# Seven experts' weights split ahead of their stage by GpSimd, and the routed products moved to VectorE

## The chip, the cores and the metric

The kernel runs on one core of a Trainium2 chip. Its time is the device time of one execution in microseconds (us); the median of three runs is given, and one further execution was taken with the hardware profiler. Five engines work side by side: TensorE (PE, its weight loads are PEld), VectorE (DVE), ScalarE (ACT), GpSimd (POOL) and SyncE (SP). Each runs its own list of instructions in order, and they wait for one another by semaphores. SP only issues transfers; here POOL issues some too.

## The reference, cut to what matters

2048 tokens of 512 values go through two layers, each a per-sequence matrix and then a feed-forward block, with a residual added:

```python
# layer 0: 2048 hidden values, low-rank terms of 8 experts, top 2 of 8
x = einsum('bct,bcd->bdt', x, weights[conditions])
for k in range(2):
    z1 = (u1 * oh_k).reshape(N, 64)
    h = gelu(x @ W1.T + b1 + z1 @ B1_rf * 2)
    u2 = einsum('nf,erf->ner', h, A2)
    y = h @ W2.T + b2 + (u2 * oh_k) @ B2_rf * 2
    res += w_topk[:, k] * y
# layer 1: 8 routed experts of 352 hidden values (top 2), a shared one of 704
g = silu(x @ w_gate[e]) * (x @ w_up[e])
out = sum_e comb[:, e] * (g @ w_down[e]) + (silu(x @ sw_gate) * (x @ sw_up)) @ sw_down
```

## The kernel before

Every matrix product is done in three products of halves: an f32 matrix is rounded to a high half (a cast to fp32r) and what is left becomes the low half (a subtraction), and high x high, high x low and low x high are summed. So each weight has to be split once on the chip: one cast and one subtraction over it.

**Layer 0** takes four super tiles `s` of 512 tokens, and for each of them 16 hidden tiles `f` of 128: 64 steps. A step of PE is the up product into `ps_h` (L1645 to L1647) and the down product into `ps_y` (L1687 to L1689), each for 512 columns and both choices `k`. ACT applies gelu (L897, L903). DVE then works in a fixed chain for each step: it adds and masks (L1202), and makes `g_hi` and `g_lo` by a cast (L1208) and a subtraction (L1210), and the same for the second choice (L1215 is its subtraction). In `s = 0` ACT casts each tile of W1 and POOL subtracts (`low_w1`, L667); both halves are stored to scratch `w1s_d` and are loaded from there for `s = 1` to `3` (704 KB a step, on SP's queue). From then until near the end of the layer POOL only issues the sequence matrices of layer 1 (`cw1`, `side_col`) in a loop.

**The shared stage** of layer 1 (some 560 to 755 us) computes the shared expert, the gate, and a table of slots: each of 39 slot tiles takes 128 tokens of one expert, by expert. `last_tile[e]` and `etab` tell which tile is of which expert. With these inputs experts 0 to 5 have 5, 4, 6, 4, 4 and 5 slot tiles, so the last tiles are 4, 8, 14, 18, 22 and 27, and experts 6 and 7 share the last eleven.

**The routed stage** (755 to 1032 us) takes one slot tile after the other. For tile `t` on PE: gate product of `t+1` into `ps_h`, transposes of the hidden tile (`turn_g`), up product of `t+1` into `ps_y`, transposes of the gathered rows of `t+2` (`turn_x`), down product. Around it:
- POOL issues `gather(t)` (L744, an indirect DMA of 128 rows of `xc_d` into one of four `xg`) and `scatter_add(t)` (L755, an indirect DMA that adds `yt` into `out`; each waits until the one before it has landed). It also does three operations a tile: `x_low` (L761), the product `rs * ru` (L769) and `g_low` (L773). A scatter is issued one tile later than its `yt` is made.
- ACT casts `xg_hi` (L1002) and copies `xg_f` beside it out of PSUM for POOL, does the silu, copies `ru` (L1016), casts `rgt_hi` (L1020) and copies `rgt_f`, and weighs the result into `yt` (L1030).
- DVE only splits experts 1 to 7: SP loads the raw weights of one (2112 KB, L610 to L614) into `e_raw`, and once the last tile of expert `e-2` is through, DVE splits them in four turns into one of the two buffers of `eg_hi`, `eg_lo`, `ed_hi`, `ed_lo` (L1477 to L1491).

The program ends when the last scatter has landed.

## Time and profile before

| | us |
|---|---|
| median of three runs (lowest, highest) | 1048.93 (1048.3, 1049.98) |
| profiled execution, its time | 1050.06 |
| profiled execution, its span | 1048.2 |

| stage | us of the span | what fills it |
|---|---|---|
| `s = 0` of layer 0, with the splits of W1 | about 40 to 155 | PE, all engines near it |
| layer 0, `s = 1` to `3` | 155 to 545 | PE, 7.39 a step |
| shared stage | 560 to 755.5 | PE |
| routed stage | 755.5 to 1031.7 | PE, 6.9 a tile |
| last scatters | 1031.7 to 1048.2 | indirect DMAs |

The profile's page gives each engine's busy time as a share of the span, then the chain of work that ended last, by engine. Busy shares are averages over stages; what a stage is worth is read in its own rows: windows give busy time by stage, and a timeline gives single instructions with the idle time before each in brackets and what ended it.

### The profile page before, as it was taken

The page shows a single profiled execution, that of the slowest core. Times are in us where ns is not written, and L with a number is a line of the kernel's source. Part 1 is how long each engine was busy: PE and PEld are TensorE (multiplying, and loading weights), DVE is VectorE, ACT ScalarE, POOL GpSimd, SP SyncE. Part 2 cuts the span into 40 slices and gives each one's busy share as a digit, 9 for nine tenths or more (in the row PEclk, how much of TensorE's full clock was granted, in tenths as well). Part 3 has the DMA queues.
Part 4 walks back from the last instruction along what each step waited for, and adds up shares of the span by engine and source line. Part 5 has one row for each costly group of instructions (what it writes and reads, how often), then busy time and mean ns, then how long its engine had stood idle before and what let it go on. Part 6 is the DMA issues. An engine that isn't in the chain of part 4 may idle for free.

```text
span 1048.2 us, 14852 instructions
## 1 busy us (share of the span) xinstructions
PE 1010.6 (96%) x4893; PEld 837.2 (80%) x4895; DVE 524.3 (50%) x886; ACT 314.4 (30%) x550; POOL 354.5 (34%) x351
## 2 busy tenths in 40 slices
PE   8899999999999999999999999999989999999993
PEld 5678887888888887888867777778778999999992
DVE  3788777455565455555566333665543314443000
ACT  3743332211121112111242010301144545454541
POOL 4123245410000000000042000022168889898873
PEclk9999999999999999999999999999999999999997
DMA  7387543443433434453444101005155665665433
GB/s 239 130 297 272 161 136 122 166 161 114 140 123 121 153 128 161 142 181 123 138 159 151 41 1 41 1 1 198 58 187 108 163 163 142 141 146 119 80 61 40
DMA packets 51322, 136.41 MB, mean 130 GB/s; under 512 B 8708, under 2 KB 10004, under 8 KB 50772
## 3 DMA queue, kind: packets, MB, share of 16 engines
q1 hardware_dynamic: 36660, 108.15, 30.1%
q0 software_dynamic: 12432, 25.71, 12.4%
q10 hardware_dynamic: 2192, 2.08, 0.7%
q8 instruction: 19, 0.31, 0.1%
q14 instruction: 19, 0.16, 0.0%
HBM read 96.85 MB, written 39.07 MB: 130 GB/s over the span
## 4 chain that ended last, share of the span: by engine, by line
PE 85%; DVE 4%; POOL 4%; DMA 2%; issue 1%; ACT 1%; ACTq 1%; PEldq 0%; POOLq 0%; PEld 0%; DVEq 0%
PE ps_y L1687 6%; PE ps_y L1689 6%; PE ps_y L1688 5%; PE ps_h L1645 5%; PE ps_h L1647 5%; PE ps_h L1646 5%; PE ps_u L1700 3%; PE ps_u L1699 3%; PE ps_h L1933 2%; PE ps_y L1933 2%; PE ps_y L1928 2%; PE ps_y L1929 2%; PE ps_y L1856 2%; PE ps_y L1857 2%; PE ps_h L1840 2%; PE ps_h L1841 2%
## 5 line engine op out<-in xcount | busy, mean ns | idle before, releaser
L1202 DVE TENSOR_TENSOR h<-h,wb 128x512 f32<-128x512 f32 x64 | 44.4, 693 | 162.6 <-ACT h L903 162.5
L897 ACT ACTIVATE h<-ps_h,bias 128x512 f32<-128x512 f32 x64 | 44.0, 689 | 235.1 <-PE ps_h L1654 235.1
L685 POOL DMA_DIRECT2D s_raw<-in_sgu x8 | 4.3, 544 | 299.9 <-DVE g_lo L1210 192.1
L1687 PE MATMUL ps_y<-w_hi,g_hi 128*128 (+1 forms) x256 | 102.2, 399 | 3.5 <-DVE g_lo L1210 3.5
L1689 PE MATMUL ps_y<-w_hi,g_lo 128*128 (+1 forms) x256 | 101.2, 395 | 0.0
L1688 PE MATMUL ps_y<-w_lo,g_hi 128*128 (+1 forms) x256 | 101.0, 395 | 0.0
L1645 PE MATMUL ps_h<-xt_hi,w_hl 128*128 128x512 f32 x256 | 100.0, 391 | 0.7 <-ACT lg_t L846 0.7
L1647 PE MATMUL ps_h<-xt_hi,w_hl 128*128 128x512 f32 x256 | 100.3, 392 | 0.0
L1646 PE MATMUL ps_h<-xt_lo,w_hl 128*128 128x512 f32 x256 | 100.2, 391 | 0.0
L1477 DVE CAST eg_hi<-e_raw 128x704 fp32r<-128x704 f32 x32 | 16.7, 581 | 138.0 <-PE ps_y L1958 125.3
L903 ACT ACTIVATE h<-ps_h,bias 128x512 f32<-128x512 f32 x64 | 43.9, 688 | 115.4 <-PE ps_h L1667 115.4
L755 POOL DMA_INDIRECT out_x<-yt,slot_tok x39 | 62.7, 1607 | 23.3 <-DMA out_x<-yt,slot_tok 12.5
L761 POOL TENSOR_TENSOR xg_lo<-xg_f,xg_hi 128x512 fp32r<-128x512 f32 x39 | 56.3, 1443 | 17.0 <-ACT xg_f L1005 14.9
L1687 PEld LDWEIGHTS ps_y<-w_hi,g_hi 128*128 128x128 f32 x256 | 48.0, 187 | 15.3 <-DVE g_lo L1210 3.5
L1215 DVE TENSOR_TENSOR g_lo<-h,g_hi 128x512 fp32r<-128x512 f32 x64 | 56.9, 888 | 2.2
L1645 PEld LDWEIGHTS ps_h<-xt_hi,w_hl 128*128 128x128 f32 x256 | 48.1, 188 | 12.2 <-ACT lg_t L846 1.2
L1689 PEld LDWEIGHTS ps_y<-w_hi,g_lo 128*128 128x128 f32 x256 | 48.1, 188 | 11.6
L1688 PEld LDWEIGHTS ps_y<-w_lo,g_hi 128*128 128x128 f32 x256 | 48.1, 188 | 11.5 <-issue 0.2
L1646 PEld LDWEIGHTS ps_h<-xt_lo,w_hl 128*128 128x128 f32 x256 | 48.1, 188 | 11.1
L1647 PEld LDWEIGHTS ps_h<-xt_hi,w_hl 128*128 128x128 f32 x256 | 48.1, 188 | 10.4
L773 POOL TENSOR_TENSOR rgt_lo<-rgt_f,rgt_hi 128x384 fp32r<-128x384 f32 x39 | 52.8, 1353 | 6.8 <-ACT rgt_f L1023 6.8
L1928 PE MATMUL ps_y<-eg_hi,xg_hi 128*128 x156 | 53.5, 345 | 0.0
(319 smaller groups left out, 2455.5 us busy)
## 6 DMA issues: line engine op xcount, KB each, us to landing
w_hl<-w1s_d SPq DMA_DIRECT2D x49, 704.0 KB, 4.1
w1s_d<-w_hl SPq DMA_DIRECT2D x16, 704.0 KB, 5.9
e_raw<-in_wgu SPq DMA_DIRECT2D x8, 1408.0 KB, 7.1
w_raw<-in_w1b SPq DMA_DIRECT2D x16, 608.0 KB, 4.7
xres<-in_x SPq DMA_DIRECT2D x16, 256.0 KB, 4.5
acc<-x_d SPq DMA_DIRECT2D x4, 1024.0 KB, 7.6
xc_d<-xc SPq DMA_DIRECT2D x4, 1024.0 KB, 4.8
e_raw<-in_wdn SPq DMA_DIRECT2D x8, 512.0 KB, 8.4
```

Of the source, the lines that this page charges most:

```text
L755: pool.indirect_dma_start(out=out, in_=yt[t % 4][:], in_offset=None, out_offset=bass.IndirectOffsetOnAxis(ap=slot_tok[:, t:t + 1], axis=0) ...
L761: nc.gpsimd.tensor_tensor(xg_lo[:].rearrange("p c n -> p (c n)"), xg_f[:], xg_hi[:].rearrange("p c n -> p (c n)").bitcast(F32), ALU.subtract)\
L773: nc.gpsimd.tensor_tensor(rgt_lo[:].rearrange("p c n -> p (c n)"), rgt_f[:], rgt_hi[:].rearrange("p c n -> p (c n)").bitcast(F32), ALU.sub ...
L1202: tt(h1[u][:], h1[u][:], wb[:, v, :], ALU.mult).then_inc(gch, 1)
L1215: tt(g1_lo[u][:], h1[u][:], g1_hi[u][:].bitcast(F32), ALU.subtract).then_inc(g1_done, 1)
L1645: mm(ps_h[:, u, :], w_chunk(u, 0, c), xt_hi[v][:, c, :], start=(c == 0), stop=False)
L1646: mm(ps_h[:, u, :], w_chunk(u, 0, c), xt_lo[v][:, c, :], start=False, stop=False)
L1647: mm(ps_h[:, u, :], w_chunk(u, 1, c), xt_hi[v][:, c, :], start=False, stop=False)
L1687: mm(ps_y[:, j, :], g_hi[u][:, cols], sl(w2_hi), start=first, **kw)
L1688: mm(ps_y[:, j, :], g_hi[u][:, cols], sl(w2_lo), start=False, **kw)
L1689: mm(ps_y[:, j, :], g_lo[u][:, cols], sl(w2_hi), start=False, **kw)
L1928: mm(o, xg_hi[:, c, :], w(eg_hi, c), start=(c == 0), stop=False)
```

## The change

- In `s = 1` to `3` of layer 0 POOL takes the weights of experts 1 to 7 in 42 units of 128 x 768 (a host-side layout `we1`, rows padded): it loads a unit (384 KB, `load_unit`), casts it (`high_unit`), stores the high half to scratch `e_d`, subtracts in place (`low_unit`) and stores the low half. There are two buffers for the high halves, and two for the raw ones, three from the ninth unit on (the two more are `u1t`, a tile of layer 0). Unit `k`'s load waits until the down product of step `16 + (k - 2)` is through, so it keeps to one unit a step; the last two stand behind the loads of the shared weights.
- In the routed stage SP loads both halves of an expert straight into the four buffers (`load_halves`, four DMAs, 4352 KB), for `e >= 2` as soon as the last tile of expert `e-2` is through, on the same semaphore that DVE's split had. Expert 1's halves are loaded before the last store of `acc`. DVE's splits of experts 1 to 7 are gone; expert 0 is split as before.
- `x_low`, the product and `g_low` go from POOL to DVE, and read PSUM: ACT's copies `xg_f`, `ru` and `rgt_f` are gone. `xg_hi` and `xg_lo` have two buffers each.
- POOL in the routed stage has gathers and scatters alone, `scatter_add(t)` right behind the wait for its own `yt`.
- PE does `turn_x(0)` in the shared stage, and `turn_x(t+2)` right behind `turn_g(t)`, ahead of the up product.
- `side_col` becomes column 65 of `cw1`: 32 DMAs in place of 64, issued among `low_w1`.

On POOL, in layer 0 behind the last `low_w1`, the loop of small loads stands before, and the shared weights follow at once:

```order
L452 DMA side_col<-in_side 64x1
L672 REGISTER_ALU
L672 COMPARE_AND_BRANCH
L685 DMA s_raw<-in_sgu 128x704 x6
L704 TENSOR_TENSOR sg_lo<-s_raw,sg_hi 128x1408
```

and now the units stand there (`pre_raw`, `u1t` hold raw units, `pre_hi` the high half, `e_d` is the scratch):

```order
L462 DMA cw<-in_cond 64x65
L715 DMA pre_raw<-in_we 128x768
L722 CAST pre_hi<-pre_raw 128x768
L724 DMA e_d<-pre_hi 128x768
L715 DMA u1t<-in_we 128x768
L728 TENSOR_TENSOR pre_raw<-pre_raw,pre_hi 128x768
L731 DMA e_d<-pre_raw 128x768
```

The pattern repeats 42 times, with the next load between the store of the high half and the subtraction.

On POOL in the routed stage, a slot tile before:

```order
L773 TENSOR_TENSOR rgt_lo<-rgt_f,rgt_hi 128x384
L769 TENSOR_TENSOR rg<-rs,ru 128x352
L761 TENSOR_TENSOR xg_lo<-xg_f,xg_hi 128x512
L744 DMA xg<-xc_d,slot_tok 128x512
L755 DMA out_x<-yt,slot_tok 2176x512
```

and now, from the stage's start:

```order
L816 DMA xg<-xc_d,slot_tok 128x512 x2
L838 MEMSET rg 128x32
L816 DMA xg<-xc_d,slot_tok 128x512 x4
L827 DMA out_x<-yt,slot_tok 2176x512
L816 DMA xg<-xc_d,slot_tok 128x512
L827 DMA out_x<-yt,slot_tok 2176x512
```

The first six gathers have no arithmetic between them, and the scatter of a tile is no longer behind the arithmetic of later tiles.

On PE in a slot tile, the end of the up product before, with the transposes of `xg` (`ident,xg`) behind it and ahead of the down product:

```order
L1929 MATMUL ps_y<-eg_lo,xg_hi 128x352
L1933 MATMUL ps_y<-eg_hi,xg_lo 128x352 x4
L1914 MATMUL ps_u<-ident,xg 128x128 x4
L1953 ISA
L1953 MATMUL ps_y<-ed_hi,rgt_hi 128x512
```

and now, where the gate product of the next tile (`ps_h`) ends:

```order
L2006 MATMUL ps_h<-eg_hi,xg_lo 128x352 x4
L2014 MATMUL ps_u<-ident,rg 128x128 x3
L1948 MATMUL ps_u<-ident,xg 128x128 x4
L2001 ISA
L2001 MATMUL ps_y<-eg_hi,xg_hi 128x352
```

The transposes of `xg` have moved ahead of the up product.

The diff, cut to its core:

```diff
+    UNITS, UW = 6, we1.shape[2] // 6
+    AHEAD = UNITS * (E - 1)
+    IN_TWO = 8
+    raw_of = [k % 2 if k < IN_TWO else (k - IN_TWO) % 3 for k in range(AHEAD)]
+    raw_used = [raw_of[:k].count(raw_of[k]) for k in range(AHEAD)]
+    e_d = scr("e_d", (E - 1, 2, UNITS, P, UW))
...
+        ahead = ExitStack()
+        sb_ahead = tensors(ahead)
+        pre_hi = [sb_ahead(f"pre_hi{u}", [P, UW], F32R)[:] for u in range(2)]
+        pre_raw = [sb_ahead("pre_raw0", [P, UW])[:], u1t[:, 0:UW], u1t[:, UW:2 * UW]]
...
-        xg_lo = sb("xg_lo", [P, DC, P], F32R)
-        xg_f = sb("xg_f", [P, DC * P])
+        xg_hi = [sb(f"xg_hi{u}", [P, DC, P], F32R) for u in range(2)]
+        xg_lo = [sb("xg_lo0", [P, DC, P], F32R)]
...
-        def load_matrix(eng, dst, k, width, which, j, h):
-
-            table = (cond0, cond1)[k]
-            off = h * SEQ if width == P else 0
-            b = eng.value_load(it_row[k][0:1, bass.ds(j * 2 + h, 1)], min_val=0, max_val=table.shape[0] // SEQ - 1)
-            eng.dma_start(dst[h * SEQ:(h + 1) * SEQ, bass.ds(j, 1), off:off + SEQ]
-                          .rearrange("p a n -> p (a n)"), table[bass.ds(b * SEQ, SEQ), :]).then_inc(which, 16)
-            if k == 1:
-                eng.dma_start(side_col[h * SEQ:(h + 1) * SEQ, bass.ds(j, 1)],
-                              side[bass.ds(b * SEQ, SEQ), :]).then_inc(which, 16)
+        def load_matrix(eng, j, h):
+
+            at = j * 2 + h
+            b = eng.value_load(it_row[1][0:1, at:at + 1], min_val=0, max_val=cond1.shape[0] // SEQ - 1)
+            eng.dma_start(cw1[h * SEQ:(h + 1) * SEQ, j, :], cond1[bass.ds(b * SEQ, SEQ), :]).then_inc(cw1_in[h], 16)
...
             def load_expert(e):
-                if e:
-                    sp.wait_ge(e_done, e)
...
-            for s in range(NS):
+            def load_halves(e):
+                b = e % 2
+                for k, (eg, ed) in enumerate(((eg_hi, ed_hi), (eg_lo, ed_lo))):
+                    sp.dma_start(eg[:, b].bitcast(F32),
+                                 e_d[e - 1, k, 0:DC, :, 0:2 * H1].rearrange("c p n -> p c n")).then_inc(half_in, 16)
+                    sp.dma_start(ed[:, b].rearrange("p c n -> p (c n)").rearrange("p (c n) -> p c n", n=UW).bitcast(F32),
+                                 e_d[e - 1, k, DC:UNITS].rearrange("c p n -> p c n")).then_inc(half_in, 16)
+
+            for s in range(NS - 1):
                 store_acc(s)
+            for u in range(2):
+                sp.wait_ge(pre_hi_st[u], 16 * (AHEAD // 2))
+            for u in range(3):
+                sp.wait_ge(pre_lo_st[u], 16 * raw_of.count(u))
+            sp.wait_ge(gu_done, NS * SH)
+            load_halves(1)
+            store_acc(NS - 1)
             for e in range(1, E):
-                load_expert(e)
+                if e >= 2:
+                    tiles = sp.value_load(last_tile[0:1, e:e + 1], min_val=0, max_val=SLOT_TILES)
+                    sp.wait_ge(ry_done, 1 + tiles)
+                    load_halves(e)
+                sp.wait_ge(half_in, 64 * e)
+                sp.wait_ge(e_done, e)
+                sp.sem_inc(e_done, 1)
...
             for f in range(FT):
                 low_w1(f, f % 2)
-            with pool.Fori(0, J) as j:
                 for h in range(2):
-                    load_matrix(pool, cw1, 1, SEQ, cw1_in[h], j, h)
-
...
+            pool.wait_ge(w1_lo_done, 2 + FT)
+            pool.wait_ge(w2_lo_done, FT)
+            pool.wait_ge(z_ok, 4)
+
+            def load_unit(k):
+                u = raw_of[k]
+                pool.wait_ge(d_done, 2 + FT + max(k - 2, 0))
+                if u == 2 and not raw_used[k]:
+                    pool.wait_ge(z_ok, 6)
+                if raw_used[k]:
+                    pool.wait_ge(pre_lo_st[u], 16 * raw_used[k])
+                at = k % UNITS * UW
+                pool.dma_start(pre_raw[u], we1[k // UNITS, :, at:at + UW]).then_inc(pre_in[u], 16)
+
+            def high_unit(k):
+                u = k % 2
+                pool.wait_ge(pre_in[raw_of[k]], 16 * (raw_used[k] + 1))
+                if k >= 2:
+                    pool.wait_ge(pre_hi_st[u], 16 * (k // 2))
+                nc.gpsimd.tensor_copy(pre_hi[u], pre_raw[raw_of[k]]).then_inc(pre_hi_done, 1)
+                pool.wait_ge(pre_hi_done, k + 1)
+                pool.dma_start(e_d[k // UNITS, 0, k % UNITS], pre_hi[u].bitcast(F32)).then_inc(pre_hi_st[u], 16)
+
+            def low_unit(k):
+                raw = pre_raw[raw_of[k]]
+                nc.gpsimd.tensor_tensor(raw.bitcast(F32R), raw, pre_hi[k % 2].bitcast(F32), ALU.subtract)\
+                    .then_inc(pre_lo_done, 1)
+                pool.wait_ge(pre_lo_done, k + 1)
+                pool.dma_start(e_d[k // UNITS, 1, k % UNITS], raw).then_inc(pre_lo_st[raw_of[k]], 16)
+
+            def units(ks):
+                for k in ks:
+                    high_unit(k)
+                    if k <= IN_TWO:
+                        load_unit(k + 1)
+                    if IN_TWO <= k < AHEAD - 2:
+                        load_unit(k + 2)
+                    low_unit(k)
+
+            shared_at = (NS - 2) * FT + 2
+            load_unit(0)
+            units(range(shared_at))
...
+            units(range(shared_at, AHEAD))
...
                     pool.wait_ge(a_done, STEPS)
+                    for u in range(3):
+                        pool.wait_ge(pre_lo_st[u], 16 * raw_of.count(u))
...
-            def x_low(t):
-                pool.wait_ge(xg_f_done, t + 1)
-                nc.gpsimd.tensor_tensor(xg_lo[:].rearrange("p c n -> p (c n)"), xg_f[:],
-                                        xg_hi[:].rearrange("p c n -> p (c n)").bitcast(F32), ALU.subtract)\
-                    .then_inc(xg_lo_done, 1)
-
-            def products(t):
-                pool.wait_ge(ru_done, t + 1)
-                if t:
-                    pool.wait_ge(rgt_done, t)
-                nc.gpsimd.tensor_tensor(rg[:, 0:H1], rs[:], ru[:], ALU.mult).then_inc(rg_done, 1)
-
-            def g_low(t):
-                pool.wait_ge(rgt_f_done, t + 1)
-                nc.gpsimd.tensor_tensor(rgt_lo[:].rearrange("p c n -> p (c n)"), rgt_f[:],
-                                        rgt_hi[:].rearrange("p c n -> p (c n)").bitcast(F32), ALU.subtract)\
-                    .then_inc(rgt_lo_done, 1)
...
             pool.wait_ge(xc_st, 16 * NS)
...
             gather(0)
             gather(1)
+            pool.wait_ge(gu_done, NS * SH)
             nc.gpsimd.memset(rg[:, H1:HC * P], 0.0).then_inc(rg_zero, 1)
-            x_low(0)
-            products(0)
-            x_low(1)
             pool.wait_ge(sy_done, NS * TPS)
             for t in range(2, 5):
                 gather(t)
             for t in range(SLOT_TILES):
-                g_low(t)
-                if t + 1 < SLOT_TILES:
-                    products(t + 1)
-                if t + 2 < SLOT_TILES:
-                    x_low(t + 2)
                 if t + 5 < SLOT_TILES:
                     gather(t + 5)
-                if t:
-                    scatter_add(t - 1)
-            scatter_add(SLOT_TILES - 1)
+                scatter_add(t)
...
-            def x_high(t, first=False):
+            def x_high(t, u):
                 act.wait_ge(xgt_done, t + 1)
-                nc.scalar.copy(xg_hi[:].rearrange("p c n -> p (c n)"), ps_u[:, 0, :]).then_inc(xg_hi_done, 1)
-                if not first:
-                    act.wait_ge(xg_lo_done, t)
-                nc.scalar.copy(xg_f[:], ps_u[:, 0, :]).then_inc(xg_f_done, 1)
+                nc.scalar.copy(xg_hi[u][:].rearrange("p c n -> p (c n)"), ps_u[:, 0, :]).then_inc(xg_hi_done, 1)
...
-            def up(t, u):
-                act.wait_ge(rup_done, t + 1)
-                nc.scalar.copy(ru[:], ps_y[:, u, 0:H1]).then_inc(ru_done, 1)
-
...
-                    up(t + 1, 1 - u)
+                g_high(t)
                 if nxt2:
-                    x_high(t + 2)
+                    x_high(t + 2, u)
                 weigh(t, n, stored)
-            x_high(0, first=True)
+            x_high(0, 0)
             silu(0, 0, first=True)
...
                 dve.wait_ge(s_hi_done, n + 1)
                 if n:
                     dve.wait_ge(z_done, 2 + STEPS)
+                else:
+                    for u in range(2):
+                        dve.wait_ge(pre_hi_st[u], 16 * (AHEAD // 2))
+                    for u in range(3):
+                        dve.wait_ge(pre_lo_st[u], 16 * raw_of.count(u))
...
-            for e in range(1, E):
-                dve.wait_ge(e_in, 48 * (e + 1))
-                if e >= 2:
-                    tiles = dve.value_load(last_tile[0:1, e:e + 1], min_val=0, max_val=SLOT_TILES)
-                    dve.wait_ge(ry_done, 1 + tiles)
-                for k in range(4):
-                    split_expert(e, e % 2, k)
+            def x_low(t, u):
+                dve.wait_ge(xg_hi_done, t + 1)
+                tt(xg_lo[u][:].rearrange("p c n -> p (c n)"), ps_u[:, 0, :],
+                   xg_hi[u][:].rearrange("p c n -> p (c n)").bitcast(F32), ALU.subtract).then_inc(xg_lo_done, 1)
+
+            def products(t, u, first=False):
+                dve.wait_ge(rs_done, t + 1)
+                dve.wait_ge(rup_done, t + 1)
+                if not first:
+                    dve.wait_ge(rgt_done, t)
+                tt(rg[:, 0:H1], rs[:], ps_y[:, u, 0:H1], ALU.mult).then_inc(rg_done, 1)
+
+            def g_low(t):
+                dve.wait_ge(rgt_hi_done, t + 1)
+                tt(rgt_lo[:].rearrange("p c n -> p (c n)"), ps_u[:, 1, 0:HC * P],
+                   rgt_hi[:].rearrange("p c n -> p (c n)").bitcast(F32), ALU.subtract).then_inc(rgt_lo_done, 1)
+
+            def slot_tile(t, u, nxt=True, nxt2=True):
+                g_low(t)
+                if nxt2:
+                    x_low(t + 2, u)
+                if nxt:
+                    products(t + 1, 1 - u)
+
+            x_low(0, 0)
+            x_low(1, 1)
...
                         slot_sums(0)
+                    if (s, j) == (NS - 1, 0):
+                        turn_x(0, 0, 16, first=True)
...
+                        pe.wait_ge(rg_done, t - 1)
...
                 if nxt:
                     gate_or_up(t + 1, 1 - u, after, 0)
                 turn_g(t)
+                if nxt2:
+                    turn_x(t + 2, x_buf, n)
                 if nxt:
                     gate_or_up(t + 1, 1 - u, after, 1)
-                if nxt2:
-                    turn_x(t + 2, x_buf, n)
                 down_routed(t, u, this)
             pe.wait_ge(rg_zero, 1)
-            turn_x(0, 0, 16, first=True)
             e = experts(0)
             gate_or_up(0, 0, e[0], 0)
+            turn_x(1, 1, 16)
```

## Rows read from the trace of the kernel before

**Rows 1.** The page: busy us (share) by engine; share of the last chain

```profile
PE 1010.6 (96%) x4893; PEld 837.2 (80%) x4895; DVE 524.3 (50%) x886; ACT 314.4 (30%) x550; POOL 354.5 (34%) x351
...
PE 85%; DVE 4%; POOL 4%; DMA 2%; issue 1%; ACT 1%; ACTq 1%; PEldq 0%; POOLq 0%; PEld 0%; DVEq 0%
```

**Rows 2.** Windows: span, busy PE, PEld, DVE, ACT, POOL, PE clock, DMA share, GB/s

```profile
190.00:427.00 237.00, 236.64 (x1030) 191.92 (x1029) 133.71 (x227) 45.93 (x69) 15.07 (x29) 1.00 0.40 136
755.48:773.44 17.96, 13.97 (x73) 11.82 (x72) 4.98 (x6) 5.79 (x12) 10.12 (x10) 0.92 0.67 224
773.00:1022.00 249.00, 246.32 (x1444) 227.25 (x1443) 73.09 (x94) 123.05 (x252) 216.57 (x177) 1.00 0.54 125
```

**Rows 3.** Timeline, layer 0: start, duration us, instruction [idle before, what ended it]

```profile
382.12 0.69 DVE L1202 TENSOR_TENSOR h<-h,wb 128x512 f32<-128x512 f32 x1 [3.72 <-ACT h L903]
...
384.03 0.69 DVE L1210 TENSOR_TENSOR g_lo<-h,g_hi 128x512 fp32r<-128x512 f32 x1
...
386.27 0.39 PE L1687 MATMUL ps_y<-w_hi,g_hi 128*128 x1
...
389.51 0.69 DVE L1202 TENSOR_TENSOR h<-h,wb 128x512 f32<-128x512 f32 x1 [3.72 <-ACT h L903]
```

**Rows 4.** Timeline, layer 0, s = 0: POOL's W1 subtraction beside DVE's subtraction

```profile
140.48 1.75 POOL L667 TENSOR_TENSOR w_hl<-w_raw,w_hl 128x640 fp32r<-128x640 f32 x1
...
140.83 1.95 DVE L1215 TENSOR_TENSOR g_lo<-h,g_hi 128x512 fp32r<-128x512 f32 x1
```

**Rows 5.** Costs by line: duration ns min/median/max, first and last start us, forms

```profile
L1215 DVE TENSOR_TENSOR g_lo<-h,g_hi x64: 691/694/1946, 52.6 to 529.2; 128x512 fp32r<-128x512 f32 x64
```

**Rows 6.** Timeline, routed stage: POOL's subtraction with DVE idle

```profile
822.80 1.28 POOL L761 TENSOR_TENSOR xg_lo<-xg_f,xg_hi 128x512 fp32r<-128x512 f32 x1
```

**Rows 7.** DMA issues: KB each, median us from issue to landing

```profile
w_hl<-w1s_d SPq DMA_DIRECT2D x49, 704.0 KB, 4.1
...
e_raw<-in_wgu SPq DMA_DIRECT2D x8, 1408.0 KB, 7.1
...
s_raw<-in_sgu POOLq DMA_DIRECT2D x8, 352.0 KB, 3.9
```

**Rows 8.** Timeline, PE, entry of the routed stage

```profile
755.48 0.60 PE L1914 MATMUL ps_u<-ident,xg 128*128 128x128 f32 x4
...
762.86 0.42 PE L1928 MATMUL ps_h<-eg_hi,xg_hi 128*128 x1 [0.92 <-ACT xg_hi L1002]
...
769.62 0.65 PE L1914 MATMUL ps_u<-ident,xg 128*128 128x128 f32 x4 [2.01 <-DMA xg<-xc_d,slot_tok]
...
773.44 0.49 PE L1928 MATMUL ps_h<-eg_hi,xg_hi 128*128 x1
```

**Rows 9.** Timeline, PE: first gate matmul of slot tiles 36, 38; last down product

```profile
1008.26 0.33 PE L1928 MATMUL ps_h<-eg_hi,xg_hi 128*128 x1
...
1021.75 0.33 PE L1928 MATMUL ps_h<-eg_hi,xg_hi 128*128 x1
...
1029.56 0.49 PE L1953 MATMUL ps_y<-ed_hi,rgt_hi 128*128 x1 [0.96 <-ACT rgt_hi L1020]
```

**Rows 10.** Timeline, the last scatters (POOL) and the last yt (ACT)

```profile
1028.37 0.69 ACT L1030 ACTIVATE yt<-ps_y,slot_w 128x512 f32<-128x512 f32 x1 [1.71 <-PE ps_y L1958]
1032.02 0.69 ACT L1030 ACTIVATE yt<-ps_y,slot_w 128x512 f32<-128x512 f32 x1 [2.21 <-PE ps_y L1958]
1033.71 1.58 POOL L755 DMA_INDIRECT out_x<-yt,slot_tok  x1 [2.81 <-DMA out_x<-yt,slot_tok]
1039.49 1.57 POOL L755 DMA_INDIRECT out_x<-yt,slot_tok  x1 [4.21 <-DMA out_x<-yt,slot_tok]
```

**Rows 11.** Timeline: a load of an expert's weights, and scatters beside it

```profile
780.49 0.37 SPq L610 DMA_DIRECT2D e_raw<-in_wgu  x1
...
783.04 1.65 POOL L755 DMA_INDIRECT out_x<-yt,slot_tok  x1 [0.31 <-issue]
...
791.84 1.57 POOL L755 DMA_INDIRECT out_x<-yt,slot_tok  x1 [2.78 <-DMA out_x<-yt,slot_tok]
```

91 lines of the change are left out of this document (49 added, 42 removed).

## Prediction

> **What bounds the kernel now.** I read the page first: PE is busy 96% of the span and carries 85% of the chain that ended last; DVE and POOL carry 4% each [rows 1]. So time is to be won only where PE waits or is slowed, and behind its last matmul. Then the windows, stage by stage. In layer 0 (190 to 427) PE is busy 236.64 of 237.00 us and POOL only 15.07: nothing to win there, something to lose. At the entry of the routed stage PE is busy 13.97 of 17.96 us, at a granted clock of 0.92; in the steady part 246.32 of 249.00, with POOL next at 216.57 [rows 2]. Last the timelines: at the entry PE waits 0.92 us for `xg_hi` and 2.01 for a gather [rows 8]; behind the last `yt`, at 1032.02, stand two scatters [rows 10].
>
> **Entry: −6.4.** The first transposes of `xg` start at 755.48, the gate product of tile 2 at 773.44 [rows 8]. This stretch holds two tiles' work less one down product (the transposes of `xg` stand for those of the hidden tile, nearly as long). A quiet tile takes 6.745 us (1008.26 to 1021.75 are two), a down product 2.46 (1029.56 to the `yt` at 1032.02) [rows 9, 10]; so 2 x 6.745 − 2.46 = 11.0 us would do, and 17.96 pass. Of the 6.9 between, 3.99 are waits (17.96 − 13.97) and 2.9 slow matmuls [rows 2], which I put down to the waits before them, as the first takes 0.49 in place of 0.33 [rows 8, 9]. The change takes the waits: `turn_x(0)` (0.60 us, still to be paid) has the shared stage behind it, `turn_x(1)` the up product, and gathers 2 to 4 have no arithmetic of POOL ahead. I take the waits and most of the slow matmuls, −6.4; bounds −3.99 and −6.9, and 0 if the gathers come no sooner.
>
> **Steady tiles: −5.5.** From 773.44 to 1021.75 are 36 tiles, 248.31 us, 6.90 each, against 6.745 in the quiet ones, where DVE splits nothing [rows 8, 9]. The rest is lost beside DVE's splits, when POOL is late with `xg_lo` or `rg`. DVE, at 73.09 of 249.00 us now [rows 2], gives up those splits and has three operations a tile instead, which even at 1 us each are 3 of 6.745; POOL's 216.57 us fall to its indirect DMAs. Of its three, `rg(t+1)` is due soonest: made behind `g_low(t)` and `x_low(t+2)`, it is needed a down and a gate product after the up product. If that cover were gone, PE would wait for it in each tile. 36 x 6.745 = 242.8, so −5.5; bounds 0 (the halves' loads slow PE as the splits did) and −6.5.
>
> **Tail: −4.65.** `yt(37)` starts at 1028.37, but its scatter at 1033.71, since POOL is a tile late; the last follows at 1039.49, 5.78 behind, of which 4.21 are a wait for the scatter before [rows 10]. Now scatter 37 can start at 1028.37 + 0.69 = 1029.06: −4.65, and the last one 5.78 behind it at 1034.84, with what follows as long as before (1039.49 to 1050.06). Bounds: −4.65, and 0 if scatters are late again; more can't be had, for the last still waits for the one before it.
>
> **Loads of the halves: +1.5.** They are 4352 KB in place of 2112. Beside the load issued at 780.49 the scatter cycle was 8.80 us (783.04 to 791.84), 3.0 above the free 5.78 [rows 10, 11]; twice the bytes may cost 6.1. In each tile of 6.745 us a scatter catches up 0.97, so 3.9 between loads four tiles apart. Lateness could grow to some 10 us by the last load, behind tile 27, which has eleven tiles, 10.6 us, to be forgotten. At the end 0 to +4.4 are left; I take +1.5. Four `yt` cover about three tiles of lateness before PE would wait. Is a load in time? 352 KB land in 3.9 us and 1408 KB in 7.1 [rows 7]: 330 KB more a us, so 4352 KB in 3.9 + 4000/330 = 16.0 us. An expert of four tiles leaves three tiles, 20.2 us. In time, by 4.2.
>
> The Trainium skill, "DMA: Bandwidth & Descriptors", on queues, rings and completion order, has each DMA engine take turns between queue rows, packet by packet. By that a scatter would hardly notice a load, and this term would be about 0. The cycle of 8.80 us speaks against it [rows 11].
>
> **Layer 0: +6.** 42 units come into 48 steps. In a step DVE's chain starts at 382.12, its low half of the first choice ends at 384.03 + 0.69 = 384.72, and PE begins the down product at 386.27: 1.55 us of slack; the next step is at 389.51, 7.39 later, with DVE idle for 3.72 [rows 3]. What does a POOL subtraction do to this? Only `s = 0` has both: POOL's starts at 140.48 for 1.75, DVE's at 140.83 takes 1.95 in place of 0.69 and ends 0.55 behind POOL's [rows 4]. It stood still meanwhile. Over layer 0 that line's median is 694 ns and the most 1946 [rows 5], so it is held in a few steps only. Alone, 512 wide, POOL's takes 1.28 us [rows 6], so 768 wide about 1.92. A hold of the whole 1.92 costs PE 1.92 − 1.55 = 0.37; if the cast holds DVE too, its own length more, which no row shows: between 0 and 1.92. Unit loads wait for a down product, so both fall at much the same place in each step. With three raw buffers I take 0.06 a unit (a full hold in one of six), 34 x 0.06 = 2; for the first eight, where a buffer must be stored before it is loaded and the place drifts, 0.5 each: 4. Sum +6. Bounds: 0, and (1.92 + 0.8 − 1.55) x 42 = +49.
>
> The Trainium skill, "SBUF — State Buffer", section "SBUF: two separate sides", speaks against this change: VectorE and GpSimd share a pair of ports, locked for a whole instruction when VectorE has two SBUF inputs or is in its fast mode, and the loser stands still. The 1.95 us agree [rows 4]. 
> POOL's pace: wait, cast 0.8 to 1.92, store issue and load issue (0.5 each), subtraction 1.92, issue 0.5: 4.3 to 5.4 us of 7.39 when loads are ahead. With two buffers the low store and next load come into the loop, each about 3.9 us as 352 KB took [rows 7], half under the other work: 7.5 to 8. What is late there the later units make good. Transfers: a step has 1152 KB more beside 704 KB (4.1 us), so 250 GB/s in 7.39 us; 136 GB/s now take a DMA share of 0.40 [rows 2, 7]. They fit; W1's tile has 3.3 us to spare. SP's queue holds no unit, and `cw1` needs fewer DMAs: nothing.
>
> **The sum.** −6.4 − 5.5 − 4.65 + 1.5 + 6 = −9.05. Against the profiled execution's 1050.06 that is 1041.0; it lies 1.13 above the median of 1048.93, on whose basis it is 1039.9. I say **1040.5**. A measurement tells 0.2%, 2.1 us, from no change.
>
> **Rivals.**
> 1. *Layer 0 costs nothing.* Both POOL operations fall where DVE is idle, and no scatter is late: −16.55, so 1032.4. For it: 3.72 idle and 1.55 slack in 7.39 us [rows 3], and a median of 694 ns even though all of `s = 0` had POOL beside it [rows 5]. Against: 3.5 us of POOL work a step must all fall into 5.3, at the right place. Chance 0.2.
> 2. *DVE is held in every step's chain, and it gets slower.* Place: layer 0, between L1202 and the end of L1210. Price 0.37 (subtraction alone) to 0.67 (0.3 of a cast too) a unit, 0.5 x 42 = 21 in place of 6: 1055. It decides from 15 us, 0.36 a unit, on. For it: rows 4 and the port rule. Against: the same rare long instructions. Chance 0.2.
> 3. *Scatters never catch up.* If a scatter beside gathers and halves cycles at 6.75 us or more, the lateness of some 8 to 12 us stays to the end: 1039.9 − 1.5 + 10 = 1048. For it: 8.80 [rows 11]. Against: 5.78 with no load [rows 10]. Chance 0.15.
> 4. *POOL ends late in layer 0.* At 8.4 us a unit it is 42 us late, two steps of it spare, and the shared weights wait: about 1065. Chance 0.05, given 4.3 to 5.4.
>
> **Chances and range.** The forecast, 1036 to 1046, has 0.4. Faster: it, rival 1 and a third of 3, less a little at its edges, 0.62. Within 0.2%: the rest of 3 near 1048 and the low edge of 2, 0.12. Slower: 0.26. The range 1031 to 1058 leaves out the far part of rival 2, rival 4 and a little below.
>
> **What would show it.** Layer 0: `h<-h,wb` 7.39 us apart or more; `g_lo` at 0.69 or up to 2.6; PE's waits for DVE ahead of the down product. POOL's two operations at 768. Routed stage: no wait over 0.2 us before the gate product of tile 2, about 11.5 us behind the first work of the stage; 6.745 us a tile; each scatter right behind its `yt` but beside a load. I am wrong if PE waits for `e_done` (a late load), if matmuls slow beside DVE's reads of PSUM, or if the free scatter cycle is above 6.7.

## The result, and the profile after

The changed kernel takes 1071.97 us (median of 4 runs, 1068.12 to 1074.33) against 1049.45 for the kernel before: a ratio of 1.0207, with a 95% interval of 1.0182 to 1.0232. The forecast was 1040.5, with 1031 to 1058 as its range. It got slower by 22.5 us. A ratio leaves out runs over 1.5% above the fastest of their kernel, below one each of numbers 4 (1077.66) and 5 (1058.9).

The page of the changed kernel: its span, then parts 1 and 4.

```profile
span 1072.7 us, 14892 instructions
...
PE 1017.5 (95%) x4894; PEld 835.8 (78%) x4895; DVE 608.2 (57%) x905; ACT 260.7 (24%) x433; POOL 383.3 (36%) x411
...
PE 76%; DVE 17%; ACT 2%; issue 2%; DMA 1%; PEldq 0%; POOLq 0%; POOL 0%; PEld 0%; DVEq 0%; ACTq 0%
```

DVE went from 4% of the last chain to 17% [rows 1]. The windows say where: the same stretch of layer 0 as before, the entry of the routed stage from the first gate product to that of tile 2, and from there to tile 38. As in rows 2, a row gives the span, busy time by engine, the granted clock, the DMA share and GB/s.

```profile
190.00:427.00 237.00, 217.39 (x919) 169.28 (x918) 180.36 (x196) 40.73 (x60) 118.27 (x135) 1.00 0.74 255
798.31:809.81 11.50, 11.40 (x69) 10.48 (x68) 4.27 (x7) 2.44 (x5) 3.80 (x4) 1.00 0.54 184
809.81:1051.01 241.20, 241.20 (x1441) 226.16 (x1440) 61.47 (x108) 72.73 (x144) 89.89 (x69) 1.00 0.69 186
```

In layer 0 PE did 919 matmuls where it did 1030 [rows 2], and DVE was busy 180 us for fewer operations than it did in 134. The clock is 1.00 in both. In the steady routed stage PE has no idle time left.

The costliest groups of DVE and PE there, from part 5:

```profile
L1758 PE MATMUL ps_y<-w_hi,g_hi 128*128 (+1 forms) x256 | 105.7, 413 | 29.5 <-DVE g_lo L1245 29.4
L1237 DVE TENSOR_TENSOR h<-h,wb 128x512 f32<-128x512 f32 x64 | 56.8, 888 | 112.1 <-ACT h L948 111.9
...
L1240 DVE TENSOR_TENSOR h<-h 128x512 f32<-128x512 f32 x64 | 65.2, 1018 | 4.4
L1243 DVE CAST g_hi<-h 128x512 fp32r<-128x512 f32 x64 | 63.5, 993 | 4.8 <-DVE h L1240 0.5
```

PE waits 29.4 us for `g_lo` ahead of the down product; it was 3.5. DVE's masking operation (`h<-h,wb`) was 0.693 us in the mean and is 0.888; its cast, 0.43 alone, is 0.993 in the mean. They run slower because they are held: they stand still while POOL works. One step shows it (POOL, DVE and the one PE row that waits):

```profile
336.39 0.54 POOL L715 DMA_DIRECT2D pre_raw<-in_we  x1 [1.63 <-DMA e_d<-pre_raw]
336.73 2.65 DVE L1237 TENSOR_TENSOR h<-h,wb 128x512 f32<-128x512 f32 x1 [1.79 <-ACT h L948]
...
336.95 1.86 POOL L728 TENSOR_TENSOR u1t<-u1t,pre_hi 128x768 fp32r<-128x768 f32 x1
...
339.41 1.66 DVE L1240 TENSOR_TENSOR h<-h 128x512 f32<-128x512 f32 x1
...
339.67 0.84 POOL L722 CAST pre_hi<-u1t 128x768 fp32r<-128x768 f32 x1
...
341.61 0.69 DVE L1245 TENSOR_TENSOR g_lo<-h,g_hi 128x512 fp32r<-128x512 f32 x1
...
342.46 0.49 PE L1758 MATMUL ps_y<-w_hi,g_hi 128*128 x1 [1.42 <-DVE g_lo L1245]
...
345.81 0.69 DVE L1237 TENSOR_TENSOR h<-h,wb 128x512 f32<-128x512 f32 x1 [2.44 <-ACT h L948]
```

DVE's first operation is 1.96 us too long, beside POOL's subtraction of 1.86; its second is 0.97 too long, beside POOL's cast of 0.84. The low half of the first choice ends 5.57 us after the chain's start (342.30 − 336.73) in place of 2.60 [rows 3], 2.97 later. Its matmul follows 0.16 behind it, at 5.73 in place of 4.15, 1.58 later. So the usable slack was 1.39 us, not 1.55. The row's 1.42 of idle time is less than 1.58 because matmuls overlap (each lasts 0.39 and they start 0.23 apart). With a slower first matmul the step lasts 9.08 us in place of 7.39. Taking the 42 steps 16 to 57 and all six DVE operations of each, the time above 0.69 and 0.43 us sums to 88.9 us; in 35 of the 42 the four operations up to the first low half are held by more than 1 us together. The last step of layer 0 starts at 566.7, against 526.0 before: layer 0 has lost 40.8 us.

The routed stage did much what the forecast said. The tail, with the first gate product of tile 38 (PE), the last two `yt` (ACT) and scatters (POOL):

```profile
1051.01 0.33 PE L2001 MATMUL ps_h<-eg_hi,xg_hi 128*128 x1
...
1057.53 0.69 ACT L1068 ACTIVATE yt<-ps_y,slot_w 128x512 f32<-128x512 f32 x1 [3.49 <-PE ps_y L2031]
1058.49 1.55 POOL L827 DMA_INDIRECT out_x<-yt,slot_tok  x1 [4.71 <-ACT yt L1068]
1061.18 0.69 ACT L1068 ACTIVATE yt<-ps_y,slot_w 128x512 f32<-128x512 f32 x1 [2.60 <-PE ps_y L2031]
1064.05 1.55 POOL L827 DMA_INDIRECT out_x<-yt,slot_tok  x1 [4.01 <-DMA out_x<-yt,slot_tok]
```

Scatter 37 starts 0.27 us behind the end of its `yt`; before it was 4.65 us behind [rows 10].

### The profile page after: what moved, and what is told of

The parts are those of the page before. It is cut to its first block, busy times and chain, and to the rows that moved or that the text cites. A ratio compares the mean times of both kernels' runs of the same rounds, so it can differ in the third digit from the quotient of the medians.

```text
span 1072.7 us, 14892 instructions
## 1 busy us (share of the span) xinstructions
PE 1017.5 (95%) x4894; PEld 835.8 (78%) x4895; DVE 608.2 (57%) x905; ACT 260.7 (24%) x433; POOL 383.3 (36%) x411
## 4 chain that ended last, share of the span: by engine, by line
PE 76%; DVE 17%; ACT 2%; issue 2%; DMA 1%; PEldq 0%; POOLq 0%; POOL 0%; PEld 0%; DVEq 0%; ACTq 0%
PE ps_y L1758 5%; PE ps_y L1759 4%; PE ps_y L1760 4%; DVE h L1240 4%; DVE g_hi L1243 4%; PE ps_h L1716 3%; PE ps_h L1718 3%; PE ps_h L1717 3%; DVE h L1237 3%; PE ps_y L2027 2%; PE ps_y L2031 2%; PE ps_y L2026 2%; PE ps_h L2006 2%; PE ps_y L2001 2%; DVE g_lo L1245 2%; PE ps_h L2002 2%
## 5 line engine op out<-in xcount | busy, mean ns | idle before, releaser
L1758 PE MATMUL ps_y<-w_hi,g_hi 128*128 (+1 forms) x256 | 105.7, 413 | 29.5 <-DVE g_lo L1245 29.4
L1237 DVE TENSOR_TENSOR h<-h,wb 128x512 f32<-128x512 f32 x64 | 56.8, 888 | 112.1 <-ACT h L948 111.9
L1605 DVE TENSOR_TENSOR rgt_lo<-ps_u,rgt_hi 128x384 fp32r<-128x384 f32 x39 | 21.7, 557 | 166.5 <-ACT rgt_hi L1061 166.5
L1240 DVE TENSOR_TENSOR h<-h 128x512 f32<-128x512 f32 x64 | 65.2, 1018 | 4.4
L1243 DVE CAST g_hi<-h 128x512 fp32r<-128x512 f32 x64 | 63.5, 993 | 4.8 <-DVE h L1240 0.5
L1068 ACT ACTIVATE yt<-ps_y,slot_w 128x512 f32<-128x512 f32 x39 | 26.9, 689 | 136.2 <-PE ps_y L2031 125.6
L805 POOL TENSOR_TENSOR oh_vals<-oh_tile,carry 128x640 fp32r<-128x640 f32 x2 | 6.5, 3244 | 139.7 <-DVE oh_tile L1500 139.7
```

The lines of the kernel that those rows point to most:

```text
L1237: tt(h1[u][:], h1[u][:], wb[:, v, :], ALU.mult).then_inc(gch, 1)
L1240: tt(h0[u][:], h0[u][:], h1[u][:], ALU.add).then_inc(gch, 1)
L1243: nc.vector.tensor_copy(g_hi[u][:], h0[u][:]).then_inc(gch, 1)
L1758: mm(ps_y[:, j, :], g_hi[u][:, cols], sl(w2_hi), start=first, **kw)
```

## The experiments

**1 to 3. Which part of the units costs.** From the changed kernel, POOL's cast, its subtraction, or both were left out; loads and stores stayed. Where the cast is out, the high buffers are zeroed once.

```diff
-                nc.gpsimd.tensor_copy(pre_hi[u], pre_raw[raw_of[k]]).then_inc(pre_hi_done, 1)
-                pool.wait_ge(pre_hi_done, k + 1)
...
-                nc.gpsimd.tensor_tensor(raw.bitcast(F32R), raw, pre_hi[k % 2].bitcast(F32), ALU.subtract)\
-                    .then_inc(pre_lo_done, 1)
-                pool.wait_ge(pre_lo_done, k + 1)
```

Neither: 

> The changed kernel with GpSimd's cast and subtraction of the units left out (the high buffers are zeroed once and stored as they are, the raw weights are stored as the low halves); all loads and stores of the units stay. Theory 1 (GpSimd's arithmetic holds VectorE in layer 0): steps of layer 0 are 7.39 us again, VectorE's operations 0.43 and 0.69 us, and the time falls by 38 to 41 us, to 1031 to 1036. Theory 2 (the 1152 KB a step of transfers, or GpSimd's issuing of them, slow layer 0): the time stays above 1060.

Cast alone: 

> The changed kernel with only GpSimd's subtraction left out (the raw weights are stored as the low halves). Theory 1: a cast of 0.84 us can hold VectorE for 0.84 us at most, under the slack of about 1.3 us before the down product, so it costs little, 1032 to 1038, though VectorE's casts beside it are stretched to about 1.05 us. Theory 1b (the cast does not hold VectorE at all): the same time, but no stretched VectorE operation. Theory 2: above 1060.

Subtraction alone: 

> The changed kernel with only GpSimd's cast left out (zeros are stored as the high halves). Theory 1: a subtraction of 1.85 us falls into VectorE's chain and costs 1.85 less 1.3 us of slack, about 0.4 to 0.6 us in most of 42 steps: 1045 to 1058. If cast and subtraction only do harm together, 1033 to 1040. Theory 2: above 1060.

| kernel | us | layer 0 later by | DVE held, 42 steps |
|---|---|---|---|
| changed kernel | 1071.97 | 40.8 | 88.9 |
| neither | 1036.66 | 2.2 | 0.1 |
| cast alone | 1040.27 | 3.1 | 9.7 |
| subtraction alone | 1062.79 | 28.8 | 69.4 |

(One run each for the last three, beside a kernel before at 1051.44, 1048.39 to 1052.66. "Later by" compares, in the profiled runs, the start of the last step's `h<-h,wb` with the kernel before.) The kernel with neither fell by 35 us, just short of the 38 to 41 expected, and far from theory 2's 1060. The arithmetic is the cost: 38.6 of 40.8 us. The transfers cost 2.2, and 1.95 of it in one step of `s = 3`, where PE waits for W1's tile. The row of the kernel with neither:

```profile
440.00 0.49 PE L1714 MATMUL ps_h<-xt_hi,w_hl 128*128 128x512 f32 x1 [1.69 <-DMA w_hl<-w1s_d]
```

One thing has to be taken out of these numbers first. In some profiled runs the granted clock falls to half (1.2 GHz) for 3.4 us. With one such stretch in the shared stage it takes 243.1 us from the last step of layer 0 to tile 2's gate product (changed kernel, numbers 2, 7, 9, 10), without one 241.5 (1, 3 to 6, 8): 1.6 us each. Layer 0's steps 16 to 63 hold none in the kernel before, the changed kernel and numbers 1, 2, 7, 8 and 9, one in 4, 5, 6 and 10, and three in 3. Each of these began in, or at most 1.2 us behind, a wait of PE of 1.8 to 3.5 us.

So about 5 of the subtraction's 28.8 us are the clock, and 2.2 the transfers: the subtraction alone costs some 22 us, within the 0.4 to 0.6 a step expected, although the time of 1062.79 is above 1058. The cast alone costs 0.9 without the transfers (DVE is held for 9.7 us, so theory 1b is out, and 1040.27 is above 1038). Together they cost 38.6, far more than the two. A cast of 0.84 us stays under the slack unless a subtraction has already used it up.

**4. Into the gap.** One wait was added, so that POOL begins a unit when DVE is through with the step:

```diff
+                pool.wait_ge(g1_done, 3 + FT + k)
                 nc.gpsimd.tensor_copy(pre_hi[u], pre_raw[raw_of[k]]).then_inc(pre_hi_done, 1)
```

> The changed kernel with one wait added: GpSimd's cast of unit k waits until VectorE's last low half of step 16 + k is made, so that cast, store issue, load issue and subtraction (about 3.9 us) fall into the 3.7 us in which VectorE is idle in each step. Theory 1: hardly an operation of VectorE is held, layer 0 costs 0 to 4 us, 1033 to 1040, faster than before the change. Rival 1b (the gap is too short for 3.9 us, and the subtraction holds the first operation of the next step): 1040 to 1050. Theory 2: above 1060.

Measured: 1069.11 (4 runs, 1061.62 to 1077.66), ratio to before 1.0159 (1.0089 to 1.0229); in the profiled run layer 0 is 30.8 us later. Neither number of theory 1 came, and against the changed kernel (1068.12 to 1074.33) the wait alone did nothing clear of noise. The trace says why (POOL and DVE, two steps):

```profile
259.19 0.84 POOL L723 CAST pre_hi<-u1t 128x768 fp32r<-128x768 f32 x1
259.27 1.05 DVE L1249 CAST g_hi<-h 128x512 fp32r<-128x512 f32 x1
...
260.34 0.54 POOL L725 DMA_DIRECT2D e_d<-pre_hi  x1 [0.30 <-POOL pre_hi L723]
...
262.92 0.69 DVE L1238 TENSOR_TENSOR h<-h,wb 128x512 f32<-128x512 f32 x1 [1.87 <-ACT h L949]
...
264.24 0.54 POOL L715 DMA_DIRECT2D u1t<-in_we  x1 [3.37 <-PE ps_u L1772]
264.38 2.57 DVE L1244 CAST g_hi<-h 128x512 fp32r<-128x512 f32 x1
264.80 1.86 POOL L729 TENSOR_TENSOR u1t<-u1t,pre_hi 128x768 fp32r<-128x768 f32 x1
```

Between cast and subtraction stands the next load, and POOL waits 3.37 us in it for PE, that is for a down product. The wait ends 1.3 us into DVE's next chain, and the subtraction follows at 264.80, beside DVE's cast, which takes 2.57 us in place of 0.43. That is one of 3 loads that wait for PE; 24 of the 42 wait for a low store to land. Either way it is the load's wait that places the subtraction. The first row shows too that a cast holds a cast: 1.05 us in place of 0.42.

**5 and 6. Subtraction ahead of the load.** The unit now casts and subtracts back to back (`split_unit`), then issues the load and both stores (`store_unit`); number 6 leaves out the wait for DVE.

```diff
                 for k in ks:
-                    high_unit(k)
+                    split_unit(k)
                     if k <= IN_TWO:
                         load_unit(k + 1)
                     if IN_TWO <= k < AHEAD - 2:
                         load_unit(k + 2)
-                    low_unit(k)
+                    store_unit(k)
```

> The changed kernel with the unit in another order: after VectorE's last low half of step 16 + k, GpSimd casts and subtracts back to back (0.84 + 1.86 us, in a gap of 3.7), and only then issues the next load and the two stores. Theory 1c (in the last run the gap did no good because the next load, which waits for a down product or for the store of a low half, stood between cast and subtraction and put the subtraction into VectorE's next chain): VectorE's operations keep 0.43 and 0.69 us in nearly all steps, layer 0 costs the 2 us of the run without arithmetic and up to 3 more, 1036 to 1041. Rival 1d (whatever the order, the loop of a unit is longer than a step of 7.39 us and drifts through VectorE's chain): 1045 to 1060.

> As the run before, without the added wait for VectorE. Theory 1c: the wait for the down product in the load now stands behind the subtraction; the cast follows it by load issue and two store issues, some 1.7 us, so the pair of 2.7 us falls on VectorE's last two operations of the step, whose results have more slack: 1038 to 1048. Rival 1d: 1050 or more.

Number 5: 1047.48 (12 runs, 1043.17 to 1058.9), ratio 0.997 (0.9943 to 0.9996), and in the profiled run (1052.11) layer 0 later by 18.7 us. Number 6, one run: 1056.68, later by 22.1. So the order was part of it, with the wait or without; what the wait adds to it isn't clear of number 5's own spread. Theory 1c promised 2 to 5 us in layer 0 and 1036 to 1041, and 1d (1045 to 1060) is nearer. The pair still started late in many steps. POOL in number 5:

```profile
319.77 1.84 POOL L726 TENSOR_TENSOR pre_raw<-pre_raw,pre_hi 128x768 fp32r<-128x768 f32 x1
325.63 0.56 POOL L715 DMA_DIRECT2D u1t<-in_we  x1 [4.01 <-DMA e_d<-u1t]
326.18 0.54 POOL L731 DMA_DIRECT2D e_d<-pre_hi  x1
326.71 0.54 POOL L733 DMA_DIRECT2D e_d<-pre_raw  x1
327.25 0.84 POOL L724 CAST pre_hi<-u1t 128x768 fp32r<-128x768 f32 x1
```

The load waits 4.01 us for the low store of the unit before, and the unit's own stores queue behind it, so that the next load will wait for those. The length of such a loop is the landing of a low store, with a median of 5.5 us from `u1t` and 5.9 from `pre_raw` in this run (page, part 6), and three issues of 0.55: 7.1 to 7.5 us and what is late besides, against a step of 7.39. Little is left to bring a late pair back into the gap.

**9 and 10. Stores ahead of the load.** From the ninth unit on, both stores come first, then the load; the low store is ahead of the high one in every unit. Number 10 again leaves out the wait for DVE.

```diff
                     split_unit(k)
-                    if k <= IN_TWO:
+                    if k < IN_TWO:
                         load_unit(k + 1)
+                    store_unit(k)
+                    if k == IN_TWO:
+                        load_unit(k + 1)
                     if IN_TWO <= k < AHEAD - 2:
                         load_unit(k + 2)
-                    store_unit(k)
```

> The kernel with both operations in the gap, with the two stores ahead of the next load from the ninth unit on, the low store first. In the run before, the load stood behind the subtraction and waited up to 4 us for the store of the unit before to land, and both stores of the unit queued behind it; so a loop of a unit took up to 8.3 us, and the pair drifted into VectorE's chain. Theory 1e (that queueing made the loop longer than a step): the pair now starts within 1 us of VectorE's last low half in units 9 to 41, layer 0 costs 5 to 9 us in place of 18.7, most of it in the first eight units, and the time is 1036 to 1042. Rival 1f (a store of 384 KB takes 5 to 6.6 us to land and that alone sets the loop): 1045 or more, and the pair late as before.

> As the run beside it, without the added wait for VectorE. If only the place of the pair in the step matters, the pair falls where the wait for a landing or a down product lets it, and layer 0 costs more than with the wait: 1042 to 1060. If the length of the loop mattered, it is as fast as with the wait.

Number 9: 1045.19 (7 runs, 1040.63 to 1047.56), ratio 0.9938 (0.9916 to 0.996): 0.6% faster than the kernel before, the clearest gain of a kernel that does all the work. Layer 0 is 9.4 us later, just above the 5 to 9 expected (theory 1e), but only 0.7 of it comes in the first eight units, where most was expected; the median missed 1036 to 1042 and meets rival 1f's 1045. DVE is held for 18.9 us in all, and in only 5 steps by over 1 us ahead of the first low half. One step of it:

```profile
346.75 0.69 DVE L1254 TENSOR_TENSOR g_lo<-h,g_hi 128x512 fp32r<-128x512 f32 x1
347.59 0.83 POOL L724 CAST pre_hi<-u1t 128x768 fp32r<-128x768 f32 x1 [2.47 <-DVE g_lo L1254]
348.50 1.85 POOL L726 TENSOR_TENSOR u1t<-u1t,pre_hi 128x768 fp32r<-128x768 f32 x1
...
351.03 0.69 DVE L1241 TENSOR_TENSOR h<-h,wb 128x512 f32<-128x512 f32 x1 [3.59 <-ACT h L952]
```

POOL waits 2.47 us for DVE, does its 2.8 us of arithmetic, and is through at 350.35, 0.68 us before the next chain. The median landing of a low store fell to 3.3 and 4.1 us, and 39 of the 42 loads show no wait. In units 9 to 41 the cast starts within 1 us of DVE's last low half in 31 of 33 units; in number 5 it was 19.

Number 10, one run, took 1057.61, with layer 0 later by 21.2 us, one stretch at half clock in it: without the wait the pair runs into DVE's chain, so the wait is needed. It also shows what sets the price. DVE is held for some 85 us, almost as long as in the changed kernel (88.9), at half the loss: 48.7 us of its holds come up to the first low half, against 76.7, and the rest fall behind it.

That the short loop is needed isn't shown. Numbers 7 and 8 below have number 5's loop, and their profiled runs lose 9.5 and 11.9 us in layer 0, number 9 9.4. In units 9 to 41 it is 8.6, 10.5 and, with a stretch at half clock, 13.0 us in numbers 7, 8 and 5, against 8.2 in number 9. The medians of 5 and 9 are 2.3 us apart, and their ranges overlap.

Of number 9's 9.4 us, 0.6 are there before the first unit, 3.8 come in the three steps at each border of super tiles, where the pair holds the first operation of the second step's chain for 1.6 us, and 1.4 in the step that waits for W1's tile. This is read from the trace and wasn't tried. The forecast's sign of a late load came here too, though not in the changed kernel: the load issued at 872.58 landed at 893.8, 21.2 us in place of 16.0, and PE waited for `e_done` (L659). Number 2 waited 1.17 us and number 3 0.66 in the same way.

```profile
894.18 0.42 PE L2005 MATMUL ps_h<-eg_hi,xg_hi 128*128 x1 [1.53 <-SPq L659]
```

**7 and 8. The routed stage's terms**, each on kernel 5.

```diff
+                if t:
+                    pool.wait_ge(ry_cp, t + 1)
+                    scatter_add(t - 1)
+            scatter_add(SLOT_TILES - 1)
-                scatter_add(t)
```

> The kernel with both operations in the gap, and the scatters one tile late again, as before the change (scatter of tile t - 1 waits for the result of tile t). If the tail term is real (-4.65), the end comes 3.6 to 4.7 us later than without it, less what the lateness behind the loads had already taken there (about 2.5 us): 1 to 4.7 us more than the kernel with both in the gap. Rival (the scatters are limited by their own landing whatever the order): no difference.

```diff
-                for k, (eg, ed) in enumerate(((eg_hi, ed_hi), (eg_lo, ed_lo))):
+                for k, (eg, ed) in enumerate(((eg_hi, ed_hi), (eg_lo, ed_lo))[:2 if e == 1 else 1]):
...
-                sp.wait_ge(half_in, 64 * e)
+                sp.wait_ge(half_in, 32 + 32 * e)
```

> The kernel with both operations in the gap, and for experts 2 to 7 only the high halves are loaded (2176 KB in place of 4352; the low halves of earlier experts stay in the buffers, so those products are wrong by the low part). If the size of the loads sets the scatters' lateness, the cycle beside a load falls from 8 to 9.4 us to about 7, and the last scatter starts up to 2.5 us sooner: 0 to 2.5 us less than the kernel with both in the gap. Rival (a load costs a scatter the same whatever its size, or the lateness is gone at the end anyway): no difference in time.

Number 7: 1060.04 (5 runs, 1050.29 to 1060.37; 1.007, 1.0048 to 1.0093) against 1047.48; number 8, one run: 1044.15. The 12.6 us between the medians of 7 and 5 are more than the scatters explain; the profiled run of 7 is its fastest, and what its others lost on top wasn't looked for. Layer 0 differs between these (later by 9.5, 18.7 and 11.9 us in the profiled runs of 7, 5 and 8), so I compare from the gate product of tile 38 to the last scatter: 20.06 us in number 7 (1019.96 to 1040.02), 14.50 in 5 (1027.34 to 1041.84), 13.28 in 8 (1020.60 to 1033.88), 17.74 in the kernel before [rows 9, 10]. Scattering a tile late costs 5.6 us, one more than expected. I put that down to the lateness behind the loads, which adds up: in number 7 the last scatters are 7 to 9 us behind their `yt`, in number 5 2 to 4. Half the bytes give back 1.2 us. Beside one load, the scatters of 8 and of 5:

```profile
807.51 1.57 POOL L829 DMA_INDIRECT out_x<-yt,slot_tok  x1 [3.97 <-ACT yt L1070]
816.16 1.58 POOL L829 DMA_INDIRECT out_x<-yt,slot_tok  x1 [5.77 <-DMA out_x<-yt,slot_tok]
821.81 1.58 POOL L829 DMA_INDIRECT out_x<-yt,slot_tok  x1 [2.76 <-DMA out_x<-yt,slot_tok]
```

```profile
814.25 1.57 POOL L829 DMA_INDIRECT out_x<-yt,slot_tok  x1 [3.97 <-ACT yt L1070]
823.15 1.58 POOL L829 DMA_INDIRECT out_x<-yt,slot_tok  x1 [6.02 <-DMA out_x<-yt,slot_tok]
831.92 1.58 POOL L829 DMA_INDIRECT out_x<-yt,slot_tok  x1 [5.89 <-DMA out_x<-yt,slot_tok]
837.49 1.58 POOL L829 DMA_INDIRECT out_x<-yt,slot_tok  x1 [2.68 <-DMA out_x<-yt,slot_tok]
```

One long cycle (8.65) with 2176 KB, two (8.90, 8.77) with 4352: a load costs a scatter about 3 us per 2100 KB. The cycle itself did not shrink to the 7 us expected; there is one of them less.

## Why the prediction was wrong

The terms of the routed stage held, and the one of layer 0 failed. All are of the profiled runs, whose difference is 1072.7 − 1048.2 = 24.5 us.

| term | forecast | measured | from |
|---|---|---|---|
| entry | −6.4 | −4.4 | gate product of tile 2: 809.81 − 40.8 = 769.0 against 773.44 |
| steady tiles | −5.5 | −7.1 | 241.20 against 248.31 |
| tail and loads | −3.15 | −4.8 | 21.7 against 26.45, tile 38's gate product to the end |
| layer 0 | +6 | +40.8 | start of the last step, 566.7 against 526.0 |

**Entry and tiles** were off by 2.0 and 1.6 us in opposite directions. The entry's waits went as forecast, and the stretch from the first gate product to that of tile 2 took 11.50 us, near the 11.0 of the sum. Its slow matmuls were read wrongly: I put 2.9 us down to the waits before them, but 1.4 are half of the 2.74 us up to 773.44 in which the clock was granted at half. In the changed kernel such a stretch came too, in the shared stage, so nothing was saved on it; that is 1.6 of the 2.0.

```profile
770.70:774.11 3.41, 3.41 (x11) 2.73 (x10) 3.38 (x5) 1.12 (x3) 2.49 (x2) 0.50 0.00 0
735.80:739.21 3.41, 3.41 (x9) 2.65 (x8) 2.45 (x2) 0.00 (x0) 3.41 (x2) 0.50 0.00 0
```

(The kernel before, then the changed one. Ahead of each, PE had waited 2.01 and 2.14 us, until 1.1 and 1.0 us before the fall.) A tile without waits takes 6.70 us, not 6.745, and every tile is one: DVE's reads of PSUM slow nothing. No PE wait for a late load shows in this run.

**Loads.** 6.1 us for one was right (3.12 + 2.99 over 5.78 in number 5). How much is left at the end depends on the run: 0 in the changed kernel, where scatter 37 is not late, 1.6 us in number 5. The landing of a load was priced too low, 16.0 us against 21.2 in number 9.

**Layer 0** is the step that failed: "With three raw buffers I take 0.06 a unit (a full hold in one of six)". The mechanism was rival 2's, and its price was under-estimated too: 40.8/42 = 0.97 a unit, not 0.5. Two things were wrong.

The frequency: holds of over 1 us fall on 35 of 42 steps. I had written that unit loads wait for a down product, so that both operations fall at much the same place in each step, and then did not ask which place. Nor is that what most loads wait for: in the changed kernel 29 of the 42 wait for a low store to land and 7 for a down product. The raw buffers were thus not ahead, as the pace of 4.3 to 5.4 us a unit took them to be. 32 of the 42 loads are issued between 0.7 us before and 2.4 us after the start of a DVE chain, and the subtraction starts 0.56 us behind each (as at 336.39 and 336.95). The loop from a low store's landing through load, subtraction and store is about a step long, so that once it meets the chain it can stay. Numbers 4, 5 and 9 show that this place was the cost, for the same 42 casts and subtractions cost 40.8 us or 9.4; that the loop locks to the chain in the way just said is my reading of the traces, not an experiment of its own.

The size: I charged the subtraction's hold less the slack, 0.37, and the cast 0.3 at most; only the bound of +49 had both in full. Where both fall in one chain the slack is used once, and the sum is 1.86 + 0.84 + the delays of handing over, less 1.39: in the step above the matmul came 1.58 late, and the step grew by 1.69.

The argument from rows 5, "so it is held in a few steps only", was a misreading. The line has 64 operations and only 16 of them belong to `s = 0`, so the median of 694 ns says nothing of these. The page of the kernel before has the mean:

```profile
L1215 DVE TENSOR_TENSOR g_lo<-h,g_hi 128x512 fp32r<-128x512 f32 x64 | 56.9, 888 | 2.2
```

It is 0.19 us above the median, 12.4 us in all, or ten operations held for 1.25. Those ten are in the first 14 steps of `s = 0`, and each of the other four has a hold too: of the cast ahead of it in two (1.79 us), of an earlier operation in two. So POOL held DVE in all 14 steps. It cost little there because twelve of the holds fell on the last two operations of the chain, behind the low half that PE waits for. Rows 5 were counted against rival 2; what they hold is a hold in every step, at a harmless place.

The port rule of the Trainium skill, "SBUF — State Buffer", section "SBUF: two separate sides", was borne out as far as the holding goes: a TensorTensor with two SBUF inputs held 1.96 us, a cast held by a subtraction (2.57 us for 0.43) and by a cast (1.05 for 0.42). The page also says that whichever starts first gets the ports. The records do not agree: DVE is held in the changed kernel even where its operation starts up to 0.45 us ahead of POOL's (0.22 at 336.73). The profile's times on POOL are rough, so this stays open. In number 10 POOL waits too: its subtraction, right behind its cast, takes 2.17 us in the median in place of 1.86. In the routed stage, where DVE reads PSUM, POOL does no arithmetic, so the exemption is not tested. From the round-robin rule (the Trainium skill, "DMA: Bandwidth & Descriptors", on queues, rings and completion order) I had worked out that loads would be about free for scatters; cycles of 8.65 to 8.90 us disagree with that working again. They don't show the rule itself wrong: what taking turns would cost a scatter I had not worked out.

Rival 1 did not come. Rival 4 did not either: POOL was through with the units in time. Of rival 3 there was nothing in the changed kernel.

## What to carry to other kernels

Filling an idle engine is priced by where its operations fall in its neighbour's chain, not by its idle share: follow each added wait to the moment that releases it, and look what the other engine does then. If two engines hold each other, give the filler a wait that opens in the neighbour's gap, keep everything that can block (loads, stores) behind the arithmetic, and check that the filler's whole loop is shorter than a step. Here the wait alone bought nothing clear of noise, the order alone some 15 us (one run), and all three together turned 2.1% slower into 0.6% faster; what the shorter loop adds to the other two isn't clear of noise. Slack is spent once per step, so a hold shorter than it is free only alone, and a hold behind the result that is waited for costs little. And look at the operations that had the neighbour beside them by themselves: a median over 64 hid fourteen held steps.
